# Loading the first adapter in two halves on one queue, with x of batches 0 and 1 sent after the warm-up memset

## The reference

```python
y = einsum('bij,bkj->bik', x, L0_cond_weight[itok_B_1_14])      # adapter of each batch, 512 x 512
logits = y[:, 107:-1, :].mean(axis=1) @ router_W.T + router_b   # 20 tokens
routing = softmax(logits)
base = y @ W.T + b
t = einsum('bsd,erd->bser', y, A)
lora = einsum('bser,eor,be->bso', t, B, routing) * 2.0
out = x + base + lora
```

## Time and profile before

| what | value |
|---|---|
| median of the runs | 74.7 us (74.18 to 76.09, 3 runs) |
| profiled execution | 74.49 us |
| its span in the trace | 72.8 us |
| PE busy | 67.7 us, 93% of the span |
| VectorE busy | 38.5 us |
| ScalarE busy | 26.4 us |
| moved by the DMA engines | 15.30 MB, mean 210 GB/s |

### The profile page before, as it was taken

One profiled execution on the slowest core, in us unless ns is written; L12 is line 12 of the kernel. 1 busy time (PEld: TensorE's weight loads), 2 busy tenths in 40 slices (PEclk: granted clock), 3 DMA queues, 4 the chain that ended last, 5 costly groups with the idle time before them and its releaser, 6 DMA issues.

```text
span 72.8 us, 1123 instructions
## 1 busy us (share of the span) xinstructions
PE 67.7 (93%) x404; PEld 52.8 (73%) x404; DVE 38.5 (53%) x99; ACT 26.4 (36%) x56; POOL 1.2 (2%) x10
## 2 busy tenths in 40 slices
PE   3997999998999999999999999999999999999930
PEld 1332244543698479998998899989789999999920
DVE  1000000225838945999974599699936098341620
ACT  0061003338258835993026997300060320240000
POOL 6000000000000000000000000000000000000000
PEclk9999999999999999999999999999999999999997
DMA  0828999999999999999724013105241320610142
GB/s 0 286 63 275 376 374 405 344 409 421 423 412 405 408 412 405 412 408 365 320 52 108 5 43 70 40 0 212 92 104 29 83 66 0 245 52 0 59 158 72
DMA packets 6774, 15.30 MB, mean 210 GB/s; under 512 B 752, under 2 KB 3312, under 8 KB 6768
## 3 DMA queue, kind: packets, MB, share of 16 engines
q1 hardware_dynamic: 6192, 14.31, 52.6%
q10 hardware_dynamic: 576, 0.92, 4.2%
HBM read 12.08 MB, written 2.10 MB: 195 GB/s over the span
## 4 chain that ended last, share of the span: by engine, by line
PE 72%; DMA 13%; SPq 9%; issue 1%; DVE 1%
PE ps_o L514 31%; DMA wc_raw<-in_wcT_dram 13%; PE ps_o L531 8%; PE ps_t L514 8%; PE ps_y L485 7%; SPq L164 4%; SPq L169 3%; PE ps_yT L496 3%; PE ps_yT L498 3%; PE ps_yT L497 3%; PE ps_y L496 3%; PE ps_y L497 3%; PE ps_y L498 2%; PE ps_yT L507 1%; SPq L189 1%
## 5 line engine op out<-in xcount | busy, mean ns | idle before, releaser
L514 PE MATMUL ps_o<-yT_hi,az_hi 128*128 128x256 f32 x64 | 18.5, 289 | 0.0
L514 PE MATMUL ps_o<-yT_hi,az_lo 128*128 128x256 f32 x64 | 17.9, 279 | 0.0
L514 PE MATMUL ps_o<-yT_lo,az_hi 128*128 128x256 f32 x64 | 17.9, 279 | 0.0
L485 PE MATMUL ps_y<-wc_raw,xT_raw 128*128 128x512 f32 x24 | 11.8, 611 | 0.8 <-DMA wc_raw<-in_wcT_dram 0.7
L514 PEld LDWEIGHTS ps_o<-yT_hi,az_hi 128*128 128x128 f32 x64 | 12.0, 188 | 0.3 <-issue 0.2
L514 PEld LDWEIGHTS ps_o<-yT_hi,az_lo 128*128 128x128 f32 x64 | 12.0, 188 | 0.3 <-issue 0.2
L514 PEld LDWEIGHTS ps_o<-yT_lo,az_hi 128*128 128x128 f32 x64 | 12.0, 188 | 0.0
L367 DVE TENSOR_TENSOR yT_lo<-ps_yT,yT_hi 128x512 fp32r<-128x512 f32 x4 | 2.7, 686 | 15.2 <-ACT yT_hi L267 15.2
L360 DVE TENSOR_TENSOR wc_lo<-wc_raw,wc_hi 128x1024 fp32r<-128x1024 f32 x8 | 9.5, 1209 | 0.0
L485 PEld LDWEIGHTS ps_y<-wc_raw,xT_raw 128*128 128x128 f32 x24 | 4.0, 191 | 7.1 <-issue 4.4
L418 DVE SCALAR_TENSOR_TENSOR o_sb<-ps_o,rest_raw,xT_raw 128x256 f32<-128x256 f32 x16 | 7.1, 477 | 3.5 <-PE ps_o L531 3.5
(11 more groups left out here) (61 smaller groups left out, 101.4 us busy)
## 6 DMA issues: line engine op xcount, KB each, us to landing
wc_raw<-in_wcT_dram SPq DMA_DIRECT2D x15, 512.0 KB, 13.9
xT_raw<-in_xT_dram SPq DMA_DIRECT2D x3, 512.0 KB, 13.4
out_dram<-o_sb SPq DMA_DIRECT2D x3, 512.0 KB, 3.3
rest_raw<-in_rest_dram SPq DMA_DIRECT2D x2, 512.0 KB, 10.8
yT_raw<-y_turn SPq DMA_DIRECT2D x14, 64.0 KB, 2.2
rest_raw<-in_rest_dram SPq DMA_DIRECT2D x1, 534.0 KB, 9.1
xT_raw<-in_xT_dram ACTq DMA_DIRECT2D x1, 512.0 KB, 3.3
out_dram<-o_sb SPq DMA_DIRECT2D x4, 128.0 KB, 1.9
```

Source lines behind the costliest of these rows:

```text
L485: last = mm(bank[:], xT_raw[:, b, c, :], wc_raw[:, b, c, :], start=(c == 0), stop=(c == C - 1))
L514: last = mm(bank[:, 0:N2], stat[:, n, c, :], mov[pair][:, c].rearrange("p b s -> p (b s)"), start=(c == 0 and k == 0), stop=(stop and c == ...
```

## The change

The first adapter now comes in two halves of two chunks, both on SP's queue, as all others do. ScalarE no longer reads an id, nor loads a chunk. The semaphore `wc01_in` and PE's wait for it are gone. ScalarE issues x of batches 0 and 1 behind its wait for `warm_ready`, which used to stand after its DMAs, in front of the first activation.

```diff
-        wc01_in = sem("wc0_chunk1_in")
...
         @block.sync
         def _(sp):
-            a = read_ids(mybir.EngineType.SP, ids)
+            _, a = nc.values_load_multi_w_load_instructions(
+                ids, engines=[mybir.EngineType.SP], min_val=0, max_val=NADAPT - 1,
+                skip_runtime_bounds_check_because="each load of an adapter checks its own address against the table")
...
-            load_chunks(sp, 0, a[0], slice(0, 1)).then_inc(wc_in[0][0], 16)
-            load_wc(0, 1)
-            load_wc(1, 0)
-            load_wc(1, 1)
+            for b in range(2):
+                load_wc(b, 0)
+                load_wc(b, 1)
             load_x(1)
...
+            act.wait_ge(warm_ready, 1)
             act.dma_start(xT_raw[:, 0:2].rearrange("p b c s -> p (b c s)"), xT[0].rearrange("p b c s -> p (b c s)"))\
                 .then_inc(x_arrived(0), 16)
-            first = read_ids(mybir.EngineType.Activation, ids[:, 0:1])
-            load_chunks(act, 0, first[0], slice(1, 2)).then_inc(wc01_in, 16)
-            act.wait_ge(warm_ready, 1)
             nc.scalar.activation(junk[:], warm[:, 0:1], ACT.Exp)
...
                 if c == 0:
                     pe.wait_ge(x_arrived(b), 16)
-                if b == 0 and c == 1:
-                    pe.wait_ge(wc01_in, 16)
-                elif c % HALF == 0:
+                if c % HALF == 0:
                     pe.wait_ge(wc_in[b][c // HALF], 16)
```

More of the change, by code:

```diff
@@ L161, in halves_split @@
             return 2 * (b - RAW) + h + 1
[L163 to L170, removed]
         def move_blocks(queue, b, parts=range(NT)):
@@ L182, in _ @@
         def _(sp):
-            a = read_ids(mybir.EngineType.SP, ids)
+            _, a = nc.values_load_multi_w_load_instructions(
+                ids, engines=[mybir.EngineType.SP], min_val=0, max_val=NADAPT - 1,
+                skip_runtime_bounds_check_because="each load of an adapter checks its own address against the table")
             def load_wc(b, h):
-                load_chunks(sp, b, a[b], half_of(h)).then_inc(wc_in[b][h], 16)
+                sp.dma_start(wc_raw[:, b, half_of(h), :].rearrange("p c o -> p (c o)"),
+                             wcT[bass.ds(a[b], 1), :, half_of(h), :].rearrange("a p c o -> (a p) (c o)"))\
+                    .then_inc(wc_in[b][h], 16)
             def load_x(g):
```

## The result

The changed kernel took 75.17 us (median of 20 runs, 74.52 to 76.22) against 74.65 for the kernel before (20 runs, 74.18 to 76.09). The ratio is 1.0062, 95% interval 1.0034 to 1.0090: about 0.5 us slower, where 0.9 us faster was forecast, and outside the range of 73.0 to 74.9. In part of the executions of either kernel PE's clock falls once near the start, which adds 1.1 to 1.4 us, and the ratios leave out the runs more than 1.5% above their kernel's fastest, but three such executions of the changed kernel (75.49 to 75.56) stay in, just under that line. Without these three the means are 74.68 us (10 runs) against 74.49 (13 runs), so that about half of the loss is theirs and 0.2 us is left.

The account below looks back on a forecast made before the run. The prediction took the DMA queue's strand to PE's wait at 17.62 us as the bound. Its terms, -0.6 and -0.3, summed to -0.9 us, giving 73.8 us against 74.7, whole range 73.0 to 74.9.

Parts of the forecast that it names:

- What bounds the kernel: Start of the kernel: PE's wait until 17.62 us for half 1 of adapter 2 moves the end by the same amount.
- Two strands: Before the wait at 17.62: PE's work ending at 17.43 and the DMA queue ending at 17.58, which binds.
- term 1: First adapter load: halves in 4 KB rows ramp the queue faster, landing 3.3 us after issue as x; -0.6 us (0 to -0.84).
- Rival C: Queue's start: row size does not feed the ramp, perhaps a register address does; 74.7 us, or 74.4; chance 0.14.
- Term 2: SP's read of eight ids: away from x's traffic it falls from 1,687 to 1,400 ns; -0.3 us (0 to -1.2).
- The bound of 480 ns: SP's id read: lower limit of its time, if reading eight ids costs what reading one does.
- Rival A: SP's id read: bound by its eight words, 172 ns each further word, so no gain there; 74.1 us; chance 0.27.
- Rival B: SP's id read falls to 480 to 700 ns, PE then binds, gain capped at 1.1; 73.6 us; chance 0.15.
- x later costs nothing: x of batches 0 and 1 issued at about 1.25, landing at 4.55, 2.3 us before PE needs it; cost 0.
- Rival D: Batch 0: half 0 lands at 7.8, PE idles, its clock stays low, costing 3.7 us; 77.8 us; chance 0.05.

Follow-up runs that it names:

- halves_only: Changed kernel with x of batches 0 and 1 issued as early as in the kernel before; ratio 0.9960 to the kernel before.
- x_after_read: Changed kernel with x of batches 0 and 1 issued by SP behind its id read, none by ScalarE; 76.96 us, one execution.
- x1_first: Changed kernel with SP loading x of batches 2 and 3 ahead of adapter 0; 77.64 us, one execution.
- contiguous: Changed kernel with the adapter table laid out half by half in DRAM, each half one contiguous 512 KB piece; ratio 0.9916 to the kernel before.
- fixed_address: Changed kernel with adapter 0's address written as a constant instead of taken from a register; 75.59 us, one execution.
- after_again: Changed kernel measured again without any edit, on the chip of the first experiments; ratio 0.9975 to the kernel before.
- x_late_only: Kernel before with only x of batches 0 and 1 issued after the wait for warm_ready, three adapter pieces kept; ratio 1.0110.
- before_warm14: Kernel before with 14 warm-ups instead of 12, nothing else; ratio 1.0007.
- split_read: Changed kernel with SP reading batch 0's id alone, issuing adapter 0's halves, then reading the other seven ids; ratio 1.0468 to the kernel before.

## Why the prediction was wrong

**What bounds the kernel** was read rightly. Two strands meet at 17.62, and everything behind them moves with it; halves_only shows the meeting point at 17.65 with PE's start at 7.82, and with contiguous halves, where half 0 is early, the chain passes by way of adapter 1's landing at 10.94.

**The step that failed first is term 1's analogy**, "if half 0 behaves as x did, it lands 3.3 us after its issue", with its reading that the queue's start is fed by rows. Half 0 landed after 4.13, 4.03, 3.96, 4.00 and 4.00 us in five profiles, 3.71 with nothing queued behind it, and about 4.9 where it was issued at 2.36. The 113 and 264 KB of the earlier trace rows were not 2 KB rows being half as much as 4 KB rows; 4 KB rows gave 111 and 266. It was the layout: an adapter half's rows lie 8 KB apart, x's follow each other. x_after_read and x1_first showed the slow stretch without any start of the queue, at 193 to 225 GB/s, and contiguous removed it. With the layout the landing comes out as the analogy had it, to a tenth of a microsecond. That 3.3 us for 512 KB equalled 3.4 for 256 KB was a coincidence of two effects; the two loads differed in rows, in bytes and in layout, and I had put it down to one.

**Term 1's size** was -0.6 us. With the halves alone the chain passes 17.65 where it passed 17.62; counted from the first issue that is -0.1 us, and the runs of halves_only give -0.3. The sum had a second fault, which the layout does not mend: it took bytes moved early for time gained at the meeting point. With contiguous halves those bytes do come early (210 KB more than with 16 warm-ups by 7.5 us, where 217 were forecast), and the chain passes 17.41, against 17.38 with the old layout and the same issue time; 17.0 was forecast. Why the later loads give the gain back stays open.

The Trainium skill (DMA: Bandwidth & Descriptors, Latency and other measured facts) has copies between DRAM tensors whose rows lie 4 MiB apart run at half rate while a pitch (the distance from row to row) of 512 KiB costs almost nothing, and advises to pad the pitch or lay tiles out contiguously. That page of the Trainium skill gives no figure for a smaller pitch; carried on downwards, its figures would make one of 8 KB harmless, which is an estimate of mine. Half 0's landing agrees with the advice and not with the estimate: here 8 KB cost about half the rate (217 against 406 GB/s), though only in the first two microseconds, since from 7.5 us on the same layout moved 311 to 422 GB/s in the changed kernel. Why it stops there no run tells.

**Rival C** came nearest in its time: next to no gain from 4 KB rows. Where half 1 landed can't be told, since PE no longer waited for it. Its reason (the address from a register) was wrong, by fixed_address; its time, 74.7, lies within half a microsecond of both measurements.

**Term 2** had the right mechanism and the wrong reach. x's data do lengthen the read: 0.90 us without them, 1.56 to 1.84 with. But I had taken the stretch before x's data as time gained. The read behaves otherwise: the loads under way when x's data set in took 0.7 to 1.0 us more each, long or short, and 0.42 us of delay leaves SP's read, from 1.68 to 2.58 even at its fastest, reaching past 2.2. It took 1,837, 1,781, 1,627, 1,602, 1,588, 1,575, 1,567 and 1,557 ns in kernels with the late x, mean 1,642, against 1,687, 1,837 and 1,834 with the early one, mean 1,786, each from one profile. The bound of 480 ns was also wrong, 897 is the read's own time. The term was -0.3 and measured -0.14, half of what the same code scatters by. Where an early and a late x were profiled on one chip, the late one was shorter by 0.06 and 0.21 us (halves_only against after_again and x_late_only) and by 0.28 (before_warm14 against contiguous), and in the first pair longer by 0.15; so a relief of the forecast size is not excluded, and the first pair did not have it. Rival A's term 2 of 0 lies near this, and its reason is wrong all the same: with no data moving one id took 469 ns and eight 897, 61 ns for each further word and not 172. Rival B's full relief was seen nowhere with x ahead of the read.

**x later costs nothing** held in the changed kernel and not by itself: x_late_only lost 1.1% and more, probably by the order of issues on two queues. The prediction didn't have to ask, since the change takes the chunk off ScalarE.

**Rival D** happened in a mild form: with PE's start at 8.0 the idle time grew to 1.9 to 2.2 us and the clock fell to 0.5 in two profiles. I priced it at 3.7 us and gave it 0.05; it costs 1.1 to 1.4 in part of the executions, 10 of 20 against 7 of 20 of the kernel before, which is no clear difference. The price was too high because the clock fell only 0.2 to 0.9 us after PE's start, and in the changed kernel's profile was back at 1.00 from about 12.3 on: batch 0's eight matmuls took 5.37 us instead of 3.67. Its landing of 7.8 was right. That the idle time is what lets the clock fall is borne out by three kernels without one fall in 12 runs each, with 16 warm-ups, with 14, and with PE's earlier start in contiguous.

What stays open is the first measurement's +0.6% against the second's -0.25% for the same kernel. Three executions with a fallen clock make up about half of the first, as said with the result; where the clock stays up it is +0.2 us against -0.2. The longest and the shortest of the read times with the late x lie 0.28 us apart for the same code on SP, so the start differs from job to job by about as much as what is left, but no run here ties the difference to it.

## What to carry to other kernels

Before a load's duration is carried over to another, all in which the two differ has to be listed: rows, bytes, layout in DRAM and what is queued beside it; here the one left out was what made the load late, and lining up the source gave the early landing that a fixed address or an empty queue behind it did not. An earlier landing of the first load is not yet a gain at a later wait: the loads in between have to be followed too. A short read that everything waits for should be over before the first bulk transfer starts to move, or start after it is in full flow; moving the transfer by half of what the read lasts bought nothing here that stands out from the scatter of the read. Warm-up work in front of a wait has to last until the data land, and its length changes with the moment at which the clock rises.

## What the runs showed of the hardware that was not expected

- Register loads from DRAM: SP's pointer before any data flowed 0.84 to 0.91 us, one id 0.47, eight ids 0.90 with nothing moving; 1.56 to 1.84 for eight when x's transfer sets in meanwhile; 0.89 for eight that start at 3.1 in x's full flow; and 5.17 us for seven that start at 4.35 with adapter 0's data, the last 1.5 us of it with 0 GB/s moving (split_read).
- A 256 KB load on ScalarE's queue, issued at 3.83 behind one load of SP's, landed after 4.2 us; issued at 4.46 behind two, after 7.6, in the longest execution of x_late_only.
- A half in 4 KB rows 8 KB apart moves at 193 to 266 GB/s in the second of its first microseconds, then at 311 to 422 in the changed kernel; the same rows in one piece move at 406 there.
- The granted clock fell to 0.50 around idle times of PE of 1.92 to 3.96 us in front of a product of batch 0, and stayed at 1.00 around 0.51, 1.00, 1.26, 1.55 and 1.73 us.
